# Causal attention: 64-row selectors, and causal masks of the maxima as 64-row matmuls of two heads

## The reference, cut to what matters

```python
def _L3_xattn_ref(q, k, v, Wq, Wk, Wv, Wo):
    NUM_HEADS, KEY_DIM, VALUE_DIM, NEG = 16, 64, 64, -1000000000.0
    B, S, _ = q.shape
    query = jnp.einsum('bse,hed->bhsd', q, Wq)
    key_p = jnp.einsum('bse,hed->bhsd', k, Wk)
    value = jnp.einsum('bse,hed->bhsd', v, Wv)
    scores = jnp.einsum('bhqd,bhkd->bhqk', query, key_p) / jnp.sqrt(jnp.asarray(KEY_DIM, jnp.float32))
    causal = jnp.tril(jnp.ones((S, S), dtype=scores.dtype))
    scores = scores + (1.0 - causal) * NEG
    alphas = jax.nn.softmax(scores, axis=-1)
    attention = jnp.einsum('bhqk,bhkd->bhqd', alphas, value)
    ...
# in the whole network: x = x + _L3_xattn_ref(_layernorm(x), ctx, ctx, ...)
```

## Time and profile before

| | us |
|---|---|
| median of 3 runs | 1970.47 (1964.48 to 1972.44) |
| the profiled execution's own time | 1968.33 |
| its span, first to last instruction | 1966.5 |
| TensorE busy, whole span | 1566.8 (80%), 12250 matmuls |
| weight loads busy | 1211.7 (62%) |
| VectorE busy | 956.5 (49%) |
| ScalarE busy | 688.7 (35%) |
| GpSimd busy | 533.5 (27%) |
| mean granted TensorE clock | 0.88 |

### The profile page before, as it was taken

How to read it: one execution, slowest core, us unless ns; L and a number is a source line. 1 busy time by engine, 2 the same in 40 slices (tenths; PEclk the granted TensorE clock), 3 DMA queues, 4 the chain that set the end, 5 groups by cost and what they waited for, 6 DMA issues and landing times. The chain is left out here.

```text
span 1966.5 us, 33821 instructions
## 1 busy us (share of the span) xinstructions
PE 1566.8 (80%) x12250; PEld 1211.7 (62%) x12250; DVE 956.5 (49%) x1948; ACT 688.7 (35%) x1527; POOL 533.5 (27%) x954
## 2 busy tenths in 40 slices
PE   4898783935788617994479989987799999999976
PEld 3565562834566516884346656654688888888765
DVE  2676261546555441212156676764354555545552
ACT  1565341312545301211146666654333222232011
POOL 2210036025434130002642555510223222232010
PEclk8798786967888758997689999998899999999886
DMA  4331363447554228883456544440200000000001
GB/s 133 83 86 22 123 275 107 146 137 170 119 119 108 80 88 298 312 316 123 119 125 144 123 109 110 110 99 2 103 7 1 6 7 7 7 1 1 1 7 44
DMA packets 89579, 195.45 MB, mean 99 GB/s; under 512 B 13808, under 2 KB 62320, under 8 KB 80848
## 3 DMA queue, kind: packets, MB, share of 16 engines
q1 hardware_dynamic: 76496, 172.94, 30.9%
q0 software_dynamic: 4608, 12.59, 2.1%
q10 hardware_dynamic: 8320, 7.87, 1.2%
HBM read 136.34 MB, written 57.02 MB: 98 GB/s over the span
## 5 line engine op out<-in xcount | busy, mean ns | idle before, releaser
L951 DVE TENSOR_REDUCE a_sb_mx<-a_mx 128x4 f32<-128x1024 f32 x192 | 234.7, 1223 | 121.2 <-PE a_mx L785 118.7
L706 ACT ACTIVATE a_sb_probs<-a_ex 128x512 f32<-128x512 f32 x384 | 208.8, 598 | 157.3 <-PE a_ex L806 156.7
L1305 DVE RECIPROCAL a_sb_rden<-a_ot 128x256 f32<-128x256 f32 x64 | 112.1, 1752 | 147.4 <-PE a_ot L1191 147.3
L806 PE MATMUL a_ex<-a_sb_QP,a_sb_KP 49*128 49x256 f32 x768 | 98.9, 334 | 39.6 <-ACT a_sb_probs L706 29.0
L249 POOL DMA_INDIRECT a_sb_landing<-f_y_slots,g_pos x48 | 46.5, 970 | 288.6 <-POOLq L143 264.8
L305 PE MATMUL a_gp<-g_ident,a_sb_xn 128*128 128x128 f32 x160 | 29.6, 314 | 117.9 <-POOL a_sb_xn L209 76.6
L806 PEld LDWEIGHTS a_ex<-a_sb_QP,a_sb_KP 49*128 49x128 f32 x768 | 60.7, 190 | 94.6 <-issue 57.2
L819 PE MATMUL a_ot<-a_sb_probs,a_sb_v 128*32 128x256 f32 x1536 | 109.3, 404 | 2.1 <-ACT a_sb_probs L706 2.1
L785 PE MATMUL a_mx<-a_sb_KP,a_sb_QP 48*128 48x256 f32 x768 | 88.2, 306 | 13.1 <-DVE a_sb_mx L951 12.4
L1134 ACT ACTIVATE a_sb_probs<-a_sc 128x512 f32<-128x512 f32 x64 | 38.2, 597 | 167.9 <-PE a_sc L1179 111.4
L305 PEld LDWEIGHTS a_gp<-g_ident,a_sb_xn 128*128 128x128 f32 x160 | 19.6, 157 | 123.9 <-issue 56.7
(11 more groups left out here) (415 smaller groups left out, 3673.0 us busy)
## 6 DMA issues: line engine op xcount, KB each, us to landing
f_sb_wb<-f_w SPq DMA_DIRECT2D x20, 2052.0 KB, 10.2
a_q_moved<-a_sb_qs SPq DMA_DIRECT2D x24, 512.0 KB, 6.0
a_sb_QP<-a_q_moved SPq DMA_DIRECT2D x48, 256.0 KB, 4.2
a_sb_kvT<-ctxT SPq DMA_DIRECT2D x32, 256.0 KB, 3.1
a_k_moved<-a_sb_ks SPq DMA_DIRECT2D x16, 512.0 KB, 3.7
a_sb_KP<-a_k_moved SPq DMA_DIRECT2D x32, 256.0 KB, 5.6
a_sb_QP<-a_q_moved SPq DMA_DIRECT2D x48, 128.0 KB, 4.5
f_x_slots<-f_sb_zero SPq DMA_DIRECT2D x1, 6144.0 KB, 20.3
```

What stands on the lines that cost most here:

```text
L706: act.activation(probs[:, group % 3, 2 * (u % 2) + par], EX[par][:], ACT.Exp, scale=scale)\
L806: op = pe.matmul(EX[par][:, t, :], KP[at:at + R + 1, b % KB, u % KM, t * P:(t + 1) * P], QP[at:at + R + 1, b % 3, u, :], start=True, stop= ...
L951: dve.tensor_reduce(pair, MX[:], AX.X, ALU.max, negate=True).then_inc(mx_read, 1)
L1305: dve.reciprocal(rden[:, n], OT[n][:, 1, :])
```

## The change

Three things are edited in `attention64`.

- `sel` and `negT` are used with 64 rows in place of 8, in the same matmul. `negT` is filled with zeros once at the start, and rows 8 to 63 and 72 to 127 of the selectors hold zeros too. VectorE drains after it.
- The identity and the mask table are stored by halves: `neg_qk` holds its first 64 query rows twice, on both halves of the partitions, and `eye` holds both 64-row halves of the identity, again on both halves of the partitions. The mask of a diagonal block is added in two matmuls of 64 rows, for the first 64 queries with all 128 keys, and for the last 64 with only the last 64 keys, by a shorter piece of the same table. The head `j` uses its own half of the array, and the two heads stand side by side in the order of issue. That makes 8 mask matmuls a unit in place of 4.
- The transfers in `loads` are 8 in place of 4.

```diff
-        eye, neg_qk = sb("eye", [P, P], BF16), sb("neg_qk", [P, P], BF16)
+        eye, neg_qk = sb("eye", [P, 2, P], BF16), sb("neg_qk", [P, P], BF16)
...
-        loads = [(neg_qk[:], io["c_neg_qk"]), (eye[:], io["c_eye"]), (wv[:], w["wv"].rearrange("(k p) n -> p k n", p=P)),
-                 (wo[:], w["wo"].rearrange("(c p) n -> p c n", p=P))]
+        halves = [slice(0, P // 2), slice(P // 2, P)]
+        loads = [(neg_qk[rows], io["c_neg_qk"][halves[0]]) for rows in halves]
+        loads += [(eye[rows, i], io["c_eye"][halves[i]]) for rows in halves for i in range(2)]
+        loads += [(wv[:], w["wv"].rearrange("(k p) n -> p k n", p=P)),
+                  (wo[:], w["wo"].rearrange("(c p) n -> p c n", p=P))]
...
                 for t in range(TT):
-                    for j in range(2):
-                        op = pe.matmul(out[:, j, t, t * P:(t + 1) * P], eye[:], neg_qk[:], start=False, stop=True,
-                                       skip_group_check=True)
+                    for half in range(2):
+                        k0 = half * (P // 2)
+                        for j in range(2):
+                            rows = slice(64 * j, 64 * j + 64)
+                            op = pe.matmul(out[:, j, t, t * P + k0:(t + 1) * P], eye[rows, half, :], neg_qk[rows, 0:P - k0],
+                                           start=False, stop=(half == 1), skip_group_check=True)
...
                     for j in range(2):
-                        rows = slice(64 * j, 64 * j + 8)
+                        rows = slice(64 * j, 64 * j + 64)
                         op = pe.matmul(out[:, j, t, q0:S], sel[rows, (2 * i + j) % 8, :], negT[rows, i // 4, q0:S],
                                        start=False, stop=True)
...
             norm_factors(dve, g, sqrt_in, sqrt_out)
+            dve.memset(negT[:].bitcast(F32), 0.0)
             for at in (0, 64):
-                op = dve.tensor_copy(sel[at:at + 8], g.ident[at:at + 8, at:at + 8].rearrange("p (j a) -> p j a", a=1)
-                                     .broadcast_to([8, 8, P]))
+                op = dve.tensor_copy(sel[at:at + 64], g.ident[at:at + 64, at:at + 8].rearrange("p (j a) -> p j a", a=1)
+                                     .broadcast_to([64, 8, P]))
             op.then_inc(sel_ready, 1)
+            dve.drain()
```

## The result

The changed kernel takes 1919.62 us (median of 4, 1915.49 to 1926.37) against 1971.45 (median of 4) of the kernel before: a ratio of 0.9747, with a 95% interval of 0.9710 to 0.9784. The forecast was 1918 in a range of 1907 to 1937. One execution of the masks alone (2613.07 us, at a granted clock of 0.545) and one of the kernel before (2081.81) were slow ones and are left out of all ratios.

What follows compares the result with a forecast made beforehand. TensorE, busy throughout each 60.89 us batch period, was taken to bound the 64-wide causal attention. Selectors 39.4, masks 8 and clock 3 sum to 50.4 us, so 1968.3 - 50.4 = 1918, range 1907 to 1937.

Steps and rivals of the forecast that it cites:

- Selectors, 1.23 a pair, 39.4 us: Score units: 64-row selector passes lose the gaps at row-count changes, a pair going from 3.20 to 1.97 us.
- Masks, 0.42 and 0.28 a pair, 1.26 a batch: Maxima units: 64-row mask pairs save 0.42 us where weighing follows, 0.28 in the three pairs before a 128-row matmul.
- The unknown: Load time of a 64-row bf16 mask, absent from the trace; taken to stay fast, as the 99 ns with 128 rows.
- The total of the masks, 8 us: Maxima units over the stage: 7.6 us from six batches and 0.5 for the first and last batch.
- The clock, 3 us: Steady stretch: two clock falls behind score units may go, 3.4 us for both, 3 taken; bounds -5 to +7.
- The start of the stage, 0: Before the first maxima: VectorE's extra fill (0.35 us) and the added transfers are covered by waits and slack, costing 0.
- What is late next: Steady batches: VectorE and ScalarE keep up, the sixth maxima unit with some 0.4 us left; nothing booked.
- The sum: Whole kernel: 39.4 + 8 + 3 = 50.4 us saved, from 1968.3 to 1918.
- Rival (a): Maxima units: masks give nothing, as the 64-row bf16 load is slow or the type change empties the array; 1927 to 1936, chance 0.20.
- (b): Score units: the selector gap belongs to its tiles or the accumulation's last pass and stays; 1960 us, chance 0.05.
- (c): Each batch: VectorE or ScalarE falls behind, 1.5 to 2.5 us of new waits; 1930 to 1938, chance 0.08.
- (d): Steady stretch: row-paired matmuls don't hold the clock; 2016 us with half the microseconds low, chance 0.03.

Runs made afterwards that it cites:

- the masks alone: The kernel before with only the mask loop, its two tables and eight transfers changed, selectors still of 8 rows: 1968.69 us, ratio 0.9991.
- the selectors alone: The kernel before with only the selectors widened from 8 to 64 rows, zero fill and VectorE's drain included, masks as before: 1925.68 us, ratio 0.9770.
- gathering the masks: The changed kernel with both units of a maxima pair doing their fp32r score passes first, then both their masks: 1919.46 us, ratio 0.9732.

## Why the prediction was right

- *Selectors, 1.23 a pair, 39.4 us.* Right. A pair went from 3.20 to 1.99, 1.21 a pair. The period of the selectors alone is 60.89 - 4.85, where 4.92 was booked. That rows, and nothing else of the pass, made the gap is shown by the runs with 32 and 40 rows, which differ in nothing else.
- *Masks, 0.42 and 0.28 a pair, 1.26 a batch.* Right in the sum, 1.23 (56.04 - 54.81), by errors that cancel, which is luck. I counted nothing for going from fp32r to bf16 in the same rows; it costs 0.10 to 0.12 a unit. And I took 0.22 for the four mask pairs of a unit, which take 0.15 (the loads from 1585.36 to the next fp32r load at 1585.51). That makes a unit 0.49 where 0.44 was booked. The pair is 1.11 for 1.09 all the same, because besides its two units it takes 0.13, where 0.21 was booked for a bare load and for emptying the array. The reading behind it was in part wrong: of the 0.32 ahead of the mask in the kernel before, which the prediction put down to rows, 0.23 stays with equal rows, and 0.11, the usual distance, is left only with equal types too (the run with masks in fp32r). So the row count made 0.09 of it, and the type 0.12. The unknown, the load of 64 bf16 rows, was decided the right way: 95 ns.
- *The total of the masks, 8 us.* About right beside the selectors: 7.4 in the steady batches (6 x 1.23), and the whole stage is 6.8 shorter than with the selectors only (465.7 and 472.5). Wrong for the part by itself. There the six periods show 2.5 and 2.3 us in its two executions, the stage 3.4 and nothing, and the wall 0.9991.
- *The clock, 3 us.* The step was right in kind, 3.4 for the two falls of the steady stretch. It was too small for the last batch: of the 10.3 us saved there I had booked 4.9 for the score pairs and about 0.3 for maxima; the other 5 go with a granted clock of 0.91 in place of 0.83. Cut into stretches of 1.5 us, the last batch shows a granted clock of 1.00 or 0.50, and something between only where a stretch holds a step: it was 0.50 for about 24 us of the last batch before and for 10 after. A low microsecond loses at most half of itself, as the prediction works out (1.69 of 3.40 us), so up to 7 us can be the clock's. With 3.4 + 5, more than 8, the clock's part is above the bound of 7 that the prediction gave it, and nearly three times the 3 of the sum: this is the term that was mis-sized.
- *The start of the stage, 0.* The fill took 0.48 (0.35 booked) and is covered: the load of the first projection still stands 1.80 until wk is there, where it was 2.13. The stretch is 0.7 longer all the same. 0.3 of that is wk's transfer, which has landed 8.5 us after the stage's first issue, and 8.2 before. Of the eleven profiled executions with eight or more transfers in `loads`, ten have 8.4 to 9.3 there and one 8.2, and the three with four transfers 8.2 or 8.3. So the small transfers may well get in its way, within the 0.5 that the prediction allowed, though no run separates them. The other 0.4 goes with the clock: the same 64 projection matmuls took 16.9 and 16.5, and the granted clock stood at 0.50 for the first 5.7 us of them, where it was 5.0. That was not tested.
- *What is late next.* No new wait in the steady stretch. The slack of the sixth unit was 0.25, where some 0.4 was booked, and gathering the masks used it up.
- *The sum.* The stage gave 54.6 where 50.4 was forecast, mostly by the clock. The medians gave 51.8. That 1919.62 lies so near to 1918 is in part luck, for the start of the stage alone moves by 14.6 us between executions. What the runs show is the mechanism: the 54.81 of every steady period, for 54.7 forecast.
- Rival (a) did not come as a whole, since the loads stay fast; its other half, a cost of the type change, is real, but is 0.10 to 0.12 a unit. (b) is excluded by the timeline. (c) by the 54.81 that holds in every period. (d) went the other way.

## What to carry to other kernels

Look at the starts of the weight loads, not at how busy TensorE is: it was at 100% while more than a third of a score unit (0.61 of 1.60 us) went on changes between row counts. Where a pass with few rows stands between passes of 64, fill it up with zero rows to 40 or 64 (33 to 39 were not run); the rows cost nothing that shows (a load of 191 ns with 64, 188 with 8), the change cost 0.2 us each time behind 256 columns and 0.15 behind 128. Where 128-row masks in bf16 stand between them, split them into two 64-row halves for two heads side by side; with masks in fp32r that split gained nothing (56.25 against 56.04 with the masks as they were). Price an edit together with its neighbours where the clock falls: the same masks were worth 0 to 3 us of the stage by themselves and about 7 behind the selectors.

## What the hardware showed that I had not expected

- A change from fp32r to bf16 operands, with the same rows, holds the next load back by 0.10 to 0.12 us (the load at 1585.36 in the changed kernel). Back from bf16 to fp32r it doesn't: the fp32r load starts at 1585.51, and the masks' matmuls are recorded from 1585.36 to 1585.70.
- The granted clock fell while TensorE's busy share was 100%, in the six steady periods always directly behind a pair of score units with gaps. None of the nine profiled executions whose score units have no gap of that kind had a fall in its six steady periods. The number of falls repeats there: 2 and 2 of six for the kernel before, 5 and 5 for the masks alone. What brings one on was not found.
- Neighbouring passes of one head share the rows and still overlap load and stream (0.117 for 256 columns), and passes of the two heads slide past each other where one has fewer columns.
